# Feed-forward weights, first batch: how the lo/hi halves of each chunk are made and copied, and when each load is issued

## The reference

```python
x = L0_attn_x                                    # (4, 512, 512)
xn = _layernorm(x)
x = x + attention(xn, Wq, Wk, Wv, Wo, biases)    # 16 heads of 32, causal, ALiBi
      + ffn(xn, gate_cp, up_cp, down_cp)
# ffn: gate_w, up_w (2048, 512), down_w (512, 2048), each rebuilt by cubic
# Catmull-Rom interpolation from 1 control point per 128.9 weights
inter = silu(xn @ gate_w.T) * (xn @ up_w.T)
return inter @ down_w.T
```

## Time and profile before

| | us |
|---|---|
| median of 3 runs (lowest to highest) | 754.38 (753.06 to 755.21) |
| the profiled execution, its own time | 754.14 |
| its span on the timeline | 752.3 |
| TensorE matmuls busy in it | 679.6 |
| VectorE, ScalarE, GpSimd busy | 467.9, 444.9, 321.9 |

### The profile page before, as it was taken

The page is one execution under the profiler, slowest core; times in us unless marked ns, Lnnn a source line. Parts: engine busy times, 40 slices in busy tenths (PEclk is TensorE's granted clock), DMA queues, the critical chain, the costliest instruction groups (busy, mean ns, idle before and its releaser), DMA issues.

```text
span 752.3 us, 13701 instructions
## 1 busy us (share of the span) xinstructions
PE 679.6 (90%) x4884; PEld 546.2 (73%) x4884; DVE 467.9 (62%) x1293; ACT 444.9 (59%) x705; POOL 321.9 (43%) x188
## 2 busy tenths in 40 slices
PE   4987889989799999799898788789999999999997
PEld 3766667868577777688776666577788888888885
DVE  6577876879877879868789887578442213223212
ACT  5477778787867977777878772444443333333321
POOL 0264545454635545544646540122243236236334
PEclk9997989999899999899999899799999999999999
DMA  8759396377575472865673957964576385244001
GB/s 311 105 79 239 61 256 107 64 139 180 81 201 79 65 105 99 144 162 68 172 110 67 326 167 204 311 224 130 162 253 226 120 243 170 74 139 142 13 1 56
DMA packets 53356, 110.15 MB, mean 146 GB/s; under 512 B 6505, under 2 KB 6761, under 8 KB 51753
## 3 DMA queue, kind: packets, MB, share of 16 engines
q1 hardware_dynamic: 51704, 106.85, 57.8%
q10 hardware_dynamic: 1584, 2.43, 1.2%
HBM read 59.32 MB, written 25.17 MB: 112 GB/s over the span
## 4 chain that ended last, share of the span: by engine, by line
PE 41%; POOL 5%; DVE 4%; issue 3%; ACT 2%; DMA 2%; ACTq 1%; SPq 0%; POOLq 0%; DVEq 0%
PE bank L1586 6%; PE bank L1588 6%; PE bank L1587 6%; PE bank L1573 3%; PE bank L1574 3%; POOL resid L1754 3%; PE bank L702 2%; PE bank L614 2%; PE bank L616 2%; PE bank L615 2%; DMA taps<-windows 2%; PE bank L688 2%; POOL in_lo L1746 1%; PE bank L719 1%; PE bank L1561 1%
## 5 line engine op out<-in xcount | busy, mean ns | idle before, releaser
L1241 POOL TENSOR_TENSOR work<-work 128x1280 f16<-128x1280 f32 x64 | 170.7, 2668 | 182.8 <-ACT work L1139 182.8
L1746 POOL TENSOR_TENSOR in_lo<-inner,in_hi 128x512 fp32r<-128x512 f32 x64 | 82.7, 1294 | 196.7 <-ACT in_hi L1653 196.7
L900 DVE CUSTOM_DVE_ANT_0 work<-bank,dist 128x128 f32<-128x128 f32 (+3 forms) x256 | 115.6, 486 | 67.1 <-PE bank L688 45.3
L1131 ACT ACTIVATE work<-work,neg_max 128x128 f32<-128x128 f32 (+3 forms) x256 | 130.3, 561 | 23.1 <-DVE neg_max L900 22.8
L1703 DVE TENSOR_TENSOR inner<-bank,silu 128x512 f32<-128x512 f32 x64 | 44.0, 688 | 130.5 <-ACT silu L1647 128.8
L1653 ACT CAST in_hi<-inner 128x512 fp32r<-128x512 f32 x64 | 39.7, 620 | 134.3 <-PE bank L1588 133.5
L702 PE MATMUL bank<-ident,work 128*128 128x128 f16 x1280 | 108.4, 230 | 9.3 <-DVE work L909 6.2
L1139 ACT CAST work<-work 128x1280 f16<-128x1280 f32 x64 | 80.6, 1259 | 60.6 <-PE bank L702 60.1
L702 PEld LDWEIGHTS bank<-ident,work 128*128 128x128 f16 x1280 | 78.0, 103 | 46.5 <-issue 33.7
L688 PE MATMUL bank<-k_stack,q_stack 96*128 96x256 f32 (+2 forms) x256 | 78.2, 381 | 25.1 <-DVE neg_max L900 19.7
L1586 PE MATMUL bank<-w_room,in_hi 128*128 128x512 f32 x256 | 100.2, 392 | 0.7 <-POOL in_lo L1746 0.7
(11 more groups left out here) (111 smaller groups left out, 1311.8 us busy)
## 6 DMA issues: line engine op xcount, KB each, us to landing
q_stack<-parts SPq DMA_DIRECT2D x48, 256.0 KB, 5.7
k_stack<-parts SPq DMA_DIRECT2D x48, 256.0 KB, 6.2
z<-xt_scratch SPq DMA_DIRECT2D x128, 88.0 KB
x_in<-x SPq DMA_DIRECT2D x32, 256.0 KB, 3.7
xt_scratch<-xt_room SPq DMA_DIRECT2D x8, 1024.0 KB, 7.0
xt_room<-xt_scratch SPq DMA_DIRECT2D x6, 1024.0 KB, 10.6
factor<-c_basis SPq DMA_DIRECT2D x5, 1024.0 KB, 11.8
taps<-windows SPq DMA_DIRECT2D x5, 1024.0 KB, 15.1
```

What stands on the lines that cost most here:

```text
L900: dve.tensor_tensor_reduce(probs[:, s % 2, OFF[i]:OFF[i] + n], score_bank[i % 2][:, 0:n], dist[:, S - n:S], -slope(s), 3.4e38, ALU.add, AL ...
L1131: e = act.activation(tile, tile, ACT.Exp, bias=neg_max[:, s % 2, i:i + 1], scale=-1.0)
L1241: pool.tensor_tensor(probs16[:, s % 2, 1, :], probs[:, s % 2, :], probs16[:, s % 2, 0, :], ALU.subtract).then_inc(lo_ready, 1)
L1746: pool.tensor_tensor(in_lo[k % 2][:, :], inner[:, k % 2, :], in_hi[:, k % 2, :].bitcast(F32), ALU.subtract).then_inc(il_ready, 1)
```

## The change

- The copies of chunks 1 to 4 are issued by SyncE and no longer by ScalarE, and each half's pair of DMAs waits only for its own half. `taps_low` too waits only for its own half.
- At the end of the attention, ScalarE casts the first half of chunk 1, then turns to the context's cast, then casts the second half; VectorE does the same with its subtractions.
- The turned input of the next batch is loaded before the first pieces and windows, right behind the moments' stores.
- `taps[3]` goes ahead of the windows of tiles 6 and 7 and ahead of the stores of sums; `taps[4]` stays behind them. The fourth store no longer stands alone behind `taps[4]`.
- One gen runs ahead of the first step and step `k` makes gen `k + 1`; tile 10 and 11 are both made in step 10.
- Chunk 2's casts move to step 0, right behind the first `silu`; the second half of chunks 2, 3, 4 is subtracted as an operation of its own, and the operations of chunk 3 stand partly one step earlier.
- SyncE issues the windows and moments of tiles 8 to 15 in one run, then chunk 3's copies, and only then the moment basis `bm`; chunk 4's copies stand between two moment stores.

```diff
--- before.py
+++ after.py
@@ -350,16 +350,16 @@
         def tiles_of(room, m, c):
             return room[m * ZR:(m + 1) * ZR, m, 4 * (c - 1):4 * c, :].rearrange("p g n -> p (g n)")
 
-        def taps_high(act, c):
+        def taps_high(act, c, some=(0, 1)):
             act.wait_ge(made[c], 7)
-            for m in range(2):
+            for m in some:
                 rows = slice(m * ZR, (m + 1) * ZR)
                 hi = coef[rows, m, :] if c == 0 else tiles_of(wgu_hi, m, c)
                 act.copy(hi, taps[c][rows, 0, :]).then_inc(made_hi[c], 1)
 
         def taps_low(eng, c, m):
 
-            eng.wait_ge(made_hi[c], 2)
+            eng.wait_ge(made_hi[c], m + 1)
             rows = slice(m * ZR, (m + 1) * ZR)
             if c == 0:
                 hi, lo = coef[rows, m, :], in_lo[0][rows, :]
@@ -369,8 +369,8 @@
 
         def copy_across(eng, c):
 
-            eng.wait_ge(made_lo[c], 2)
             for m in range(2):
+                eng.wait_ge(made_lo[c], m + 1)
                 own, other = slice(m * ZR, (m + 1) * ZR), slice((1 - m) * ZR, (2 - m) * ZR)
                 if c == 0:
                     eng.dma_start(coef[other, m, :].bitcast(F32), in_lo[0][own, :].bitcast(F32)).then_inc(dup_ld[0], 16)
@@ -1069,11 +1069,11 @@
                 dve.wait_ge(ql_ready, 8 * B)
                 for m in range(2):
                     taps_low(dve, 0, m)
+        taps_low(dve, 1, 0)
         ctx_low(B - 1, KC - 1)
+        taps_low(dve, 1, 1)
         taps_op(dve, 2, 0)
         add_residual(B - 1, 0)
-        for m in range(2):
-            taps_low(dve, 1, m)
         add_residual(B - 1, 1)
         for n in range(1, 4):
             taps_op(dve, 2, n)
@@ -1217,10 +1217,10 @@
             if s == H + 2:
                 copy_across(act, 0)
                 act.wait_ge(s_full, 4 * H * B)
-                taps_high(act, 1)
+                taps_high(act, 1, (0,))
         ctx_high(B - 1, KC - 1)
+        taps_high(act, 1, (1,))
         act.activation(warm[:], ident[0:1, 0:1], ACT.Silu)
-        copy_across(act, 1)
 
     def attention_gpsimd(pool):
         def inverse_std(b, n):
@@ -1395,29 +1395,31 @@
             for e in range(2):
                 sp.dma_start(mom_d[2 * (B - 1) + e, :, 8 * m:8 * m + per, :],
                              parts[0:NG * per, 2 * (m % 2) + e, :].bitcast(F32)).then_inc(mom_sv[m % 2], 16)
+        sp.wait_ge(xt_st, 32 * B)
+        load_turned(sp, 1)
         sp.wait_ge(lo_ready, H * B)
         load_pieces(sp, 0)
         sp.wait_ge(pt_full, QT * H * B)
-        sp.wait_ge(xt_st, 32 * B)
         sp.wait_ge(pad_st, 16)
         for g in range(4):
             load_windows(sp, 0, g)
         sp.wait_ge(mom_sv[0], 64)
         sp.wait_ge(mom_sv[1], 32)
         load_moments(sp, 0, 0)
+        copy_across(sp, 1)
         load_pieces(sp, 1)
-        load_turned(sp, 1)
         load_factor(sp, 3)
         sp.wait_ge(av_full, H * B)
-        for g in range(4, 8):
+        for g in range(4, 6):
+            load_windows(sp, 0, g)
+        sp.wait_ge(pj_full, pj_total(("o", QT - 1), B - 1))
+        load_taps(sp, 3)
+        for g in range(6, 8):
             load_windows(sp, 0, g)
         load_moments(sp, 0, 1)
-        for q in range(QT - 1):
+        for q in range(QT):
             store_sum(B - 1, q)
-        sp.wait_ge(pj_full, pj_total(("o", QT - 1), B - 1))
-        load_taps(sp, 3)
         load_taps(sp, 4)
-        store_sum(B - 1, QT - 1)
 
     ended = [0, 0, 0]
     for q in range(QT):
@@ -1432,13 +1434,13 @@
 
 
 MOM_STEPS = (8, 9)
-GEN_FRONT = {k: k + 2 for k in range(MOM_STEPS[0] + 1)}
-GEN_BACK = {k: k + 1 for k in range(MOM_STEPS[1] + 1, NG - 1)}
+GEN_FRONT = {k: k + 1 for k in range(MOM_STEPS[0] + 1)} | {MOM_STEPS[1] + 1: MOM_STEPS[1] + 1}
+GEN_BACK = {-1: 0} | {k: k + 1 for k in range(MOM_STEPS[1] + 1, NG - 1)}
 
 
 def ffn_order():
 
-    order = [("gen", 0, 0, 1), ("gen", 1, 0, 1)]
+    order = [("gen", GEN_BACK[-1], 0, 1)]
     turn = 0
     for k in range(STEPS):
         t, g = divmod(k, NG)
@@ -1459,9 +1461,9 @@
     return order + [("down", k, 0, None) for k in range(STEPS - LAG, STEPS)]
 
 
-TAPS = {1: [(2, 7)], 2: [(3, 0), (3, 1)], 3: [(3, 2), (3, 3)], 4: [(3, 4), (3, 5), (3, 6)], 5: [(3, 7), (4, 0)],
-        6: [(4, 1), (4, 2)], 7: [(4, 3), (4, 4)], 8: [(4, 5), (4, 6)], 9: [(4, 7)]}
-HIGHS = {0: 2, 4: 3, 8: 4}
+TAPS = {1: [(2, 7), (2, 8)], 2: [(3, 0), (3, 1)], 3: [(3, 2), (3, 3), (3, 4)], 4: [(3, 5), (3, 6)],
+        5: [(3, 7), (3, 8), (4, 0)], 6: [(4, 1), (4, 2)], 7: [(4, 3), (4, 4)], 8: [(4, 5), (4, 6)], 9: [(4, 7), (4, 8)]}
+HIGHS = {4: 3, 8: 4}
 ORDER = ffn_order()
 MOM_TILES = ((0, 1), (2,))
 
@@ -1652,12 +1654,12 @@
                 after_down(act, k - 2)
             act.copy(in_hi[:, k % 2, :], inner[:, k % 2, :]).then_inc(ih_ready, 1)
 
-        for g in range(2):
-            down_start(g)
-            down_high(g)
-        for kind, n, half, _ in ORDER[2:]:
+        down_start(0)
+        for kind, n, half, _ in ORDER[1:]:
             if kind == "gu":
                 gated(n)
+                if n == 0:
+                    taps_high(act, 2)
                 if n - 1 in GEN_BACK:
                     down_high(GEN_BACK[n - 1])
                 if n in GEN_FRONT:
@@ -1668,8 +1670,6 @@
                     down_start(GEN_BACK[n])
                 if n in HIGHS:
                     taps_high(act, HIGHS[n])
-                if n - 1 in HIGHS:
-                    copy_across(act, HIGHS[n - 1])
             elif kind == "mom":
                 moment_high(n, half)
 
@@ -1710,10 +1710,8 @@
                 dve.tensor_tensor(resid[:, i, :], sum_bank[i][:, :], resid[:, i, :], ALU.add
                                   ).then_inc(sum_ready, 1)
 
-        for g in range(2):
-            merge(g)
-            down_low(g)
-        for kind, n, half, _ in ORDER[2:]:
+        merge(0)
+        for kind, n, half, _ in ORDER[1:]:
             if kind == "gu":
                 multiply(n)
                 if n - 1 in GEN_BACK:
@@ -1724,8 +1722,7 @@
                     if i < 7:
                         taps_op(dve, c, i)
                     else:
-                        taps_low(dve, c, 0)
-                        taps_low(dve, c, 1)
+                        taps_low(dve, c, i - 7)
                     if at == 0 and n in GEN_FRONT:
                         down_low(GEN_FRONT[n])
                 if n in GEN_FRONT and n not in TAPS:
@@ -1805,20 +1802,22 @@
                 sp.nop(nofuse=True)
                 sp.dma_start(out_t[QT * BATCHES[t] + i], resid[:, i, :]).then_inc(out_st[i], 16)
 
+        copy_across(sp, 2)
         for q in range(QT):
             sp.wait_ge(res_st[q], 16 * B)
         sp.dma_start(factor[4][:], c_factor[4]).then_inc(chunk_ld[4], 16)
         load_pieces(2)
-        for g in range(8, 12):
-            load_windows(0, g)
-        load_moments(0, 2)
+        for q in (2, 3):
+            for g in range(4 * q, 4 * q + 4):
+                load_windows(0, g)
+            load_moments(0, q)
+        copy_across(sp, 3)
         sp.dma_start(bm[:].bitcast(F32).rearrange("p k e n -> p (k e n)"), moment_d).then_inc(bm_ld, 16)
-        for g in range(12, NG):
-            load_windows(0, g)
-        load_moments(0, 3)
         load_pieces(3)
-        for m in range(3):
-            store_moment(1, m)
+        store_moment(1, 0)
+        store_moment(1, 1)
+        copy_across(sp, 4)
+        store_moment(1, 2)
         for t in range(1, B):
             if t == 1:
                 for g in range(4):
```

## The result

| us | before | after |
|---|---|---|
| median of 20 runs each, on one chip (lowest to highest) | 754.63 (751.39 to 759.56) | 750.89 (748.74 to 755.31) |
| the profiled execution, its own time | 754.14 | 749.17 |
| its span | 752.3 | 747.4 |
| TensorE matmuls busy in it | 679.6 | 674.6 |
| VectorE, ScalarE, GpSimd busy | 467.9, 444.9, 321.9 | 467.9, 445.0, 323.1 |

The ratio is 0.9955 (95%: 0.9938 to 0.9971): 3.7 us faster by the medians, 744.0 was forecast. The change does what it is for, at about a third of the gain.

A forecast was written before the change was run, and what follows sets the result against it. TensorE was taken to lose 16.6 of 49.33 us before step 8 to stalls (DMA copies, merges, `inner`) and slow clock. Step 8 11.4 earlier, plus 0.9 for one gen, nets -10.5: 744 us, range 740.7 to 749.5.

The forecast's parts named there:

- Part 1: Context's cast at the attention's end: one cast fewer ahead of it wins 0.15 us, out of 0 to 0.62.
- Part 2: Chunk 1's copies before step 0: queue just about empty at 460.9, landing in 4 us; the 2.41 stall goes.
- Part 3: Steps 0 to 4: three stalls totalling 3.35 us replace 1.50 + 2.41 + 2.48 and the slow clock; step 4 ready at 484.15.
- Part 4: Chunk 2's copies before step 4: 7.14 MB at 273 GB/s land at 486.2, so step 8 starts at 504.4.
- Part 5: SyncE's chain to chunk 3's copies: `factor[4]` near 481, copies landed at 504.1; with slow-clock odds step 8 at 505.2.
- The sum: Step 8 from 516.62 to 505.2 gives -11.4, one gen behind it +0.9: net -10.5 us, median 744.
- At nothing: Items priced at zero: ScalarE's freed queue (inside the walk), VectorE's operations, `bm`, chunk 4's copies, gen 10's wait of about 0.5.
- The queue in order: Rival: ring drains at 242 GB/s, chunk 2's copies land at 489.5, clock falls, step 8 at 509.3: 748 us; chance 17.
- Misses its first aim: Rival: chunk 1's copies still land at 473 behind turned input, slow clock again, step 8 at 510.6: 749 us; chance 5.
- nothing waits: Rival: copies and SyncE's chain land with TensorE's walk, step 8 at 502.35: 741 us; chance 15.
- VectorE or the clock: Rival: thin first steps slow the clock or three-operation steps delay `inner`, one 2.8 us spell more: 747 us; chance 8.
- slower: Rival: crowd lasts until 495, chunk 2's copies land at 497, chunk 3's at 518.2 after late `factor[4]`: 757 us; chance 5.

The follow-up runs named there:

- e1: The changed kernel with chunk 2's four copies issued by ScalarE in step 2 instead of SyncE: 749.16 us, ratio 0.9930.
- e2: The changed kernel with the 1 MB load of taps 4 issued behind chunk 2's copies instead of ahead of them: 746.10 us, ratio 0.9913.
- g1: e2 with chunk 3's copies and the basis `bm` both ahead of the windows of tiles 12 to 15: 744.49 us, ratio 0.9853.
- g3: The same kernel as e2, run once more on another chip: 746.47 us, ratio 0.9907.
- g4: The changed kernel itself, unedited, timed again on g3's chip: 750.81 us, ratio 0.9946.
- h1: The changed kernel with SyncE holding `factor[4]` and everything after it until chunk 2's copies have landed: timed once, 753.37 us.
- h2: The changed kernel with the window loads of tiles 6 and 7 (0.36 MB) moved behind chunk 2's copies: timed once, 749.80 us.
- e3: The changed kernel with the turned input (2 MB) loaded at its old place, behind the second pieces: 753.19 us, ratio 0.9990.
- h4: g1 with the turned input loaded later, behind chunk 2's copies, `factor[4]` and the third pieces: 745.95 us, ratio 0.9878.
- f2: f1 with the gens leading by two tiles again, as before the change: 752.11 us, ratio 0.9958.
- f1: e2 with chunk 3's copies ahead of the windows of tiles 12 to 15, but `bm` still behind those windows: 751.70 us, ratio 0.9967.
- f4: The changed kernel with chunk 1's casts again ahead of the context's cast and its subtractions behind the first residual addition: timed once, 753.79 us.
- h3: g1 with chunk 1's casts and subtractions undivided, as in the kernel before: 744.76 us, ratio 0.9877.

## Why the prediction was wrong, point by point

- **What bounds the kernel** was right: between the mark and step 8 the stalls are of DMA copies, of `inner` and of merges, and the change moves them as named. A microsecond won at step 8 was one at the end: step 8 came 4.4 earlier, and less the 0.9 for the gen still to be made that is 3.5; measured 3.4. One reading was wrong: "The first matmul shows the level". After the stall of 2.09 in the kernel before, the first matmul took 0.47, and yet the clock granted over that step was 0.64 (the third number from the end):

```profile
495.30:500.00 4.70, 4.69 (x14) 3.74 (x15) 3.27 (x4) 1.37 (x3) 1.28 (x1) 0.64 0.74 288
```

So the 7.0 us lost there besides the stalls are three slow spells, not two. The 2.8 us at which the prediction prices one of them is worked out from the earlier trace rows: 6.45 us for 16 matmuls at a granted clock of 0.69, where 0.2275 each make 3.64; the clock granted from 473.4 to 477.4 was 0.50.
- **Part 1** was to win 0.15 and won nothing: the waits are 1.40 and 0.39, in all 1.79 where 1.73 was. The miss is 0.2 us.
- **Part 2, chunk 1's copies: here the first step failed,** "so the queue is just about empty at 460.9". It took a DMA share of 0.45 for 55% of free room and filled it with 2.1 MB to the brim. Before, that stretch moved 12.3 x 131 = 1.61 MB; with the turned input 3.71 MB have to pass. After, 11.9 x 284 = 3.38 MB did: by this estimate 0.33 MB were carried over. The copies landed at +9.6 where +6 to +7 was said, and step 0 waited 1.08. In the other executions of kernels that are the same up to there (e1, e2, g1, g3, g4, h1, h2) it waited 1.06 to 3.09. The cost is 1.7 us here and up to 3.7, against the +8.1 said for step 0; the stall of 2.41 with its slow clock did go. Without the turned input ahead (e3, h4) they land in 3.5 to 4.3 us, so the 4 us said for a free queue were right. That left-over bytes alone delay them isn't shown: the turned input itself had landed by 456.2, 3.1 us before the first copy was issued, and the first copy landed at +5.0, as in e3 (+4.9); only the later ones are late.
- **Part 3, the thin first steps,** was right. Its 0.08 us for each handover lies inside the 0.04 to 0.10 of the trace before (gen 0's last matmul ends at 468.36, ScalarE's copy runs from 468.40 to 468.98, VectorE's merge from 469.08 to 469.80, gen 1 starts at 469.86). Where no copy is late, in h4, step 0 stands at +8.5 (said +8.1), the stalls are 0.60, 0.70 and 1.19 (said 0.75, 1.05 and 1.55) and step 4 is at +24.6 (said +24.2). Its sentence that "each is shorter than the shortest after which the clock fell" held after the change (granted clock 1.00 from 468.2 to 479.8), and not in e2, e3 and g4 (below).
- **Part 4, chunk 2's copies, is the step that failed by size.** Said: 7.14 MB at 273 GB/s from 460.0, landed at 486.2, +26.2. Measured: +31.7, 5.5 us more. The queue began on them 0.8 us later against the mark (459.30). It then took 30.9 us instead of 26.2. By h1, where nothing else follows, 7.5 MB passed and not 7.14, 1.3 us more at 273 GB/s; that makes 27.4 us, and h1 took 30.2: the 2.8 us between I put down to the end, in which the share falls from 0.74 to 0.05 while copies are outstanding. (0.7 us more in the changed kernel's profile are within what executions differ by.) The sum divided bytes by a mean rate; it left out the carry-over and the slow end of a crowd: the time from the last bytes to the landing and, if my reading of h1 holds, an uneven load of the engines. That the bytes ahead are the main cause, and the ring they stand on the smaller one, is shown by e2 and g3 (1 MB less: 4 us earlier) against e1 (another ring: 1.7).
- **Part 5, SyncE's chain.** The last of the sums landed at +26.3 (issued at 473.1, 11.7 us to landing) and `factor[4]` went at +26.4, where +20.4 and +21.0 were said: the same queue, the same error. From there to chunk 3's copies 16.8 us passed, exactly as said. They landed at +49.9, 2.2 ahead of step 8, and only where step 4 is early (e2, g3) do they become the wait. The slow clock after the stall at step 4 cost 2.2 us: 20.36 to step 8, where 18.2 would do. It was priced at 1.6, an estimate that no run shows, made from the 2.8 us of slow clock in the earlier trace rows; 0.8 of it stood in the sum.
- **The sum:** step 8 at +52.2 instead of +45.2, 7.0 us late, of it 5.6 at step 4 and 1.4 by the clock. The median is 6.9 above the forecast.
- **At nothing:** right for ScalarE's copies. The basis `bm` was in time in this change, as said; it became a wall only where it was moved back (f2's profile; f1 is as slow). Gen 10's wait for the moments was 0.50 here.
- **The rivals.** "The queue in order" (748) named the stall: copies at 489.5, slow clock, step 8 at 509.3. In the frame of the kernel before, the copies came at 491.7 and step 8 at 512.2, beyond even that; the median of 750.89 lies outside the range (740.7 to 749.5). Its lower rate of 242 GB/s was the one to take: 248 was measured in h1 with the end of the queue's work counted. "Misses its first aim" was excluded by step 0, "nothing waits" by the stall before step 4, "VectorE or the clock" by the full clock and stalls of at most 1.22 up to step 3 (the spell it names did come in the second profile, g4, after a stall of 1.20), "slower" by `factor[4]`, 8.7 us ahead of where it was the earlier trace rows against the mark, at the point which it named.

Open: how much of the 2.8 us at the end is an uneven load and how much the last 1.9 us, in which hardly anything moved (h2 was too small an edit to tell); and why copies issued 0.9 to 1.5 us later land as early or earlier (f4, h3).

## What to carry to other kernels

Look in each queue for small transfers that gate an engine, and add up everything issued before them, the bytes left over from the stretch before included; then move what is needed later behind them: one 1 MB load taken out from ahead of four copies of 128 KB gave 3.0 to 4.3 us (mean, median), about as much as the whole change. Divide by the rate measured with the end of a crowd (248 GB/s in h1, where 273 was taken), and count the time until the landing is seen. When such a wait is gone, ask at once which transfer is next to be late, here `bm`: f1 and f2 lost 5 us by it, and g1 won 7 over f1 by having `bm` ahead of eight window loads.

## What the runs showed of the hardware that was not expected

- The DMA share of 0.45 was not 55% of room in which other transfers cost nothing (chunk 1's last copy landed at +7.0 and +7.4 without the 2.1 MB there, in h4 and e3, and at +9.6 with them), and a share under 1 didn't mean that the queue was short: in h1 it was 0.74 and 0.65 for 4 us in which `taps[4]` and at least three copies of 128 KB were outstanding, the last with 4 us to go at their end.
- The last 1.9 us before the landing of h1's last copy moved 17 GB/s. The same 128 KB copy took 2.2 us at the least (g1, chunk 3) and 14.1 at the most (e3, chunk 2).
- The same stall of 1.20 us in front of step 2 left TensorE at the full clock in some executions (0.50 for the next matmul and a granted clock of 1.00 over the step, after the change, in e1 and f4) and was followed by a lower clock in others (0.75 in e2, 0.79 in e3, 0.80 in g4, with 0.64, 0.64 and 0.69 granted over the 4.7 us from that matmul on); the two profiles of the changed kernel itself differ in this. In g4 the slow spell cost little, since a DMA was waited for soon after: it was paid out of that wait (3.77 instead of 5.76 us).
- The attention ends at a time that differs by up to 6 us between executions of nearly the same code. Single profiles can be compared only from a mark behind it.
